# A six-layer decoder on one core: layer d's DRAM round trip and GpSimd's block inversion cut into more segments, with new work orders

## What is computed

```python
A = jnp.where(strict_lo, kb @ jnp.swapaxes(k, -1, -2), 0.0)
Tinv = solve_triangular(eye + A, eye, lower=True, unit_diagonal=True)
u = Tinv @ v
w = Tinv @ kb
# then a scan over the chunks: u_i - w_i @ S, q_i @ S + attn @ u_i, S + k_i^T @ u_i
```

## Time and profile before

| | |
|---|---|
| time, median of 3 runs | 3648.71 us (3646.90 to 3649.24) |
| the profiled execution, its own time | 3649.02 us |
| its span, first to last instruction | 3647.3 us |
| PE busy | 3133.5 us, 86% of the span |
| DVE busy | 2402.2 us, 66% |
| ACT busy | 1395.9 us, 38% |
| POOL busy | 358.3 us, 10% |
| mean granted TensorE clock | 0.893 |

### The profile page before, as it was taken

How to read it: one execution, slowest core, us unless ns; L and a number is a source line. 1 busy time by engine, 2 the same in 40 slices (tenths; PEclk the granted TensorE clock), 3 DMA queues, 4 the chain that set the end, 5 groups by cost and what they waited for, 6 DMA issues and landing times.

```text
span 3647.3 us, 49503 instructions
## 1 busy us (share of the span) xinstructions
PE 3133.5 (86%) x18500; PEld 2337.8 (64%) x18500; DVE 2402.2 (66%) x5671; ACT 1395.9 (38%) x2889; POOL 358.3 (10%) x710
## 2 busy tenths in 40 slices
PE   4788989898888989889898988989898898998765
PEld 2466767576576757667576675757667675776552
DVE  5436667585766758576675857667576775857674
ACT  2334433434444343443434343333434334342321
POOL 1002001010100101010010101001010010102110
PEclk7799899999999989999899999999999998998876
DMA  3434333234323323432342343224234322341201
GB/s 102 87 84 105 78 88 68 76 71 88 85 59 90 82 69 81 85 84 54 78 103 68 82 84 82 56 76 100 74 71 89 88 57 76 81 95 48 48 12 24
DMA packets 592813, 275.94 MB, mean 76 GB/s; under 512 B 464808, under 2 KB 555072, under 8 KB 592576
## 3 DMA queue, kind: packets, MB, share of 16 engines
q1 hardware_dynamic: 490176, 138.53, 20.1%
q10 hardware_dynamic: 102400, 134.23, 12.0%
HBM read 156.55 MB, written 14.68 MB: 47 GB/s over the span
## 4 chain that ended last, share of the span: by engine, by line
PE 54%; DVE 22%; ACT 8%; issue 6%; DMA 4%; POOL 3%; SPq 2%; ACTq 0%; DVEq 0%; POOLq 0%
PE bank L885 20%; PE bank L1089 7%; PE bank L960 6%; PE bank L937 5%; ACT pt_f L1349 3%; DVE region L1966 3%; DMA qT_f<-rest_f 2%; PE bank L920 2%; ACT split_f L1360 2%; DVE nm_f L1706 2%; PE bank L1171 2%; PE bank L1250 2%; SPq L696 2%; PE bank L952 1%; DVE yc L1890 1%
## 5 line engine op out<-in xcount | busy, mean ns | idle before, releaser
L1349 ACT ACTIVATE pt_f<-bank 128x512 f32<-128x512 f32 x768 | 418.0, 596 | 356.2 <-PE bank L937 352.3
L885 PE MATMUL bank<-xTc,c_w 128*128 128x256 f32 x2048 | 522.6, 407 | 7.8 <-DVE yc L1890 6.7
L1089 PE MATMUL bank<-c_w,c_hb 128*128 128x256 f32 x2048 | 512.0, 397 | 1.6 <-ACT c_hb L1478 0.4
L885 PEld LDWEIGHTS bank<-xTc,c_w 128*128 128x128 f32 x2048 | 404.6, 204 | 76.7 <-DVE yc L1890 10.9
L1706 DVE TENSOR_REDUCE nm_f<-bank 128x2 f32<-128x512 f32 x512 | 315.3, 683 | 206.9 <-PE bank L920 206.1
L1089 PEld LDWEIGHTS bank<-c_w,c_hb 128*128 128x128 f32 x2048 | 395.2, 200 | 64.1 <-ACT c_hb L1478 8.9
L1966 DVE SCALAR_TENSOR_TENSOR region<-vpad,cols,region 128x256 f32<-128x256 f32 x1024 | 425.4, 486 | 0.0
L937 PE MATMUL bank<-qT_f,kT_f 102*128 102x256 bf16 (+1 forms) x1536 | 305.4, 317 | 110.4 <-ACT pt_f L1349 42.2
L1478 ACT ACTIVATE c_hb<-bank,cols 128x256 f32<-128x256 f32 x512 | 214.6, 471 | 339.3 <-PE bank L885 338.8
L937 PEld LDWEIGHTS bank<-qT_f,kT_f 102*128 102x128 bf16 (+1 forms) x1536 | 121.9, 104 | 309.7 <-ACT pt_f L1349 138.9
L960 PE MATMUL bank<-pt_f,v_f 128*32 128x256 f32 x3072 | 235.8, 436 | 0.0
(11 more groups left out here) (309 smaller groups left out, 5060.2 us busy)
## 6 DMA issues: line engine op xcount, KB each, us to landing
c_w<-in_c_w ACTq DMA_DIRECT2D x256, 512.0 KB, 5.0
gram_scratch<-region SPq DMA_DIRECT2D x32, 256.0 KB, 2.3
x<-in_x SPq DMA_DIRECT2D x16, 256.0 KB, 5.7
x<-in_ctx SPq DMA_DIRECT2D x16, 256.0 KB, 5.9
ctxb<-in_ctx SPq DMA_DIRECT2D x16, 256.0 KB, 2.7
out_dram<-x SPq DMA_DIRECT2D x16, 256.0 KB, 2.2
qT_f<-split_f SPq DMA_TRANSPOSE x192, 3.4
kT_f<-split_f SPq DMA_TRANSPOSE x192, 3.4
```

What stands on the lines that cost most here:

```text
L885: mm = pe.matmul(out_ap, l, r, start=(i == 0), stop=(i == len(pairs) - 1))
L1089: mm = pe.matmul(PS[use][:, t * D:(t + 1) * D], c_hb[:, k, t * P:(t + 1) * P], c_w2[:, e % W_SLOTS, k, :], start=(k == 0), stop=(k == HC - 1))
L1349: act.activation(dst, PS[use].rearrange("p (c s) -> p c s", c=c), func, **kw).then_inc(*PS.drained(use))
```

## The change

Six new segment names. On SP `d_blocks` is divided into `d_blocks` (store A) and `d_fetch` (read the blocks back), `d_place` into `d_place` (store the inverse) and `d_begin` (read it into place). On POOL the inversion is divided into `d_blocks` (identity) and `d_solve0` to `d_solve3` (four columns each, the last with three). No instruction is added or taken away. All lists in `ORDER` but those of DVE in step 0, and of SP and POOL in steps 0 and 1, are new.

```diff
-TWO = ([... "d_gram", "d_blocks", "d_grams"]
-       + ["d_fir0", "d_place", "d_fir1", "d_fir2", "d_fir3"]
+TWO = ([... "d_gram", "d_blocks", "d_grams", "d_fetch", "d_solve0", "d_solve1"]
+       + ["d_fir0", "d_solve2", "d_solve3", "d_place", "d_begin", "d_fir1", "d_fir2", "d_fir3"]
...
     ("sync", None, """
-e_in e_turnq e_turnk e_again a_norm a_turnq d_blocks a_turnk d_place f_apply b_turnq b_turnk b_again
+e_in e_turnq e_turnk e_again a_norm a_turnq d_blocks d_fetch a_turnk d_place d_begin f_apply b_turnq b_turnk b_again
...
     ("sync", 16, """    (and the same in 17)
-e_in e_turnq e_turnk e_again d_blocks d_place f_apply
+e_in e_turnq e_turnk d_blocks e_again d_fetch d_place d_begin f_apply
...
     ("gpsimd", None, """
-a_norm e_res d_norm d_blocks f_res a_res d_out d_res c_res b_res
+d_norm a_norm d_blocks e_res d_solve0 d_solve1 d_solve2 d_solve3 f_res a_res d_out d_res c_res b_res
...
     ("tensor", None, """     (the places that differ)
-... e_score2a e_score2b e_weigh1 e_score3a c_down1b e_score3b e_weigh2 e_weigh3 d_token e_out c_up2a
+... e_score2a c_down1b e_score2b e_weigh1 e_score3a d_token e_score3b e_weigh2 e_weigh3 e_out c_up2a
-c_up2b a_norm c_down2a a_proj c_down2b f_in
+c_up2b a_norm c_down2a c_down2b a_proj f_in
-b_proj c_down5a c_down5b d_twb5 c_up6a d_one6 d_two6 d_scan0 c_up6b
+b_proj c_down5a d_twb5 d_one6 c_down5b d_two6 c_up6a d_scan0 c_up6b
...
     ("scalar", None, """
-e_score1b e_score2a e_score2b d_silu e_weigh1 e_score3a e_score3b e_weigh3 d_token
+e_score1b d_silu e_score2a e_score2b e_weigh1 e_score3a e_score3b d_token e_weigh3
-a_part1 f_up1 a_part2 c_up3a
+a_part1 f_up1 c_up3a a_part2
...
     ("vector", None, """
-e_max0 d_proj e_max1 e_max2 e_max3 e_shift c_down0b d_conv
+e_max0 e_max1 e_max2 e_max3 e_shift d_proj c_down0b d_conv
-a_rope d_norm d_gram c_down2b f_up0
+a_rope c_down2b d_norm d_gram f_up0
-f_res d_fir2 f_apply d_fir3 d_one4 d_fir4 c_down4b a_out b_ctx d_two4 a_res
+f_res d_fir2 d_fir3 f_apply d_one4 d_fir4 a_out d_two4 b_ctx c_down4b a_res
-d_two5 b_part1 b_part2 d_twb5 c_down5b d_fir6 d_sums b_max0 b_max1
+d_two5 b_part1 d_twb5 b_part2 d_fir6 c_down5b b_max0 d_sums b_max1
...
     ("vector", 16, """
-e_out e_res e_apply c_down4b f_in d_one4 d_fir4
+e_out c_down4b e_res d_one4 e_apply f_in d_fir4
     ("tensor", 16, """
-e_out c_down4a c_down4b c_up5a c_up5b d_one4
+e_out c_up5a d_one4 c_up5b d_two4
...
+                yield "d_fetch"
                 sp.wait_ge(*d_gram_out(b))
...
+                yield "d_begin"
                 sp.wait_ge(*d_zero(b))
...
-                pool.wait_ge(*d_blocks_in(b))
                 for j in range(BB - 1):
+                    if j % 4 == 0:
+                        yield f"d_solve{j // 4}"
+                    if j == 0:
+                        pool.wait_ge(*d_blocks_in(b))
```

More of the change, by code:

```diff
@@ L158 @@
     ("tensor", 1, """
[L159 to L163, removed]
+c_in a_norm c_gate a_proj c_comb c_up0a c_up0b c_down0a c_down0b c_up1a c_up1b c_down1a c_down1b c_up2a a_score0a
+c_up2b a_score0b a_score1a a_score1b a_weigh0 a_score2a a_score2b a_weigh1 a_score3a c_down2a a_score3b a_weigh2
+a_weigh3 c_down2b a_out b_in b_ctx a_res c_up3a c_up3b b_x b_proj c_down3a c_down3b c_up4a c_up4b c_down4a c_down4b
+c_up5a c_up5b b_max0 c_down5a c_down5b b_max1 c_up6a b_max2 c_up6b b_max3 c_down6a c_down6b b_again c_up7a c_up7b
+b_score0a b_score0b b_score1a b_score1b b_weigh0 b_score2a c_down7a b_score2b b_weigh1 b_score3a c_down7b b_score3b
 b_weigh2 b_weigh3 b_out b_res
@@ L166 @@
     ("tensor", 2, """
[L167 to L172, removed]
+d_in d_proj a_norm c_in c_gate a_proj c_comb c_up0a c_up0b c_down0a c_down0b c_up1a c_up1b d_token c_down1a c_down1b
+c_up2a c_up2b d_chan c_down2a c_down2b d_gram a_score0a c_up3a a_score0b c_up3b a_score1a d_grams a_score1b a_weigh0
+c_down3a a_score2a c_down3b a_score2b a_weigh1 a_score3a c_up4a a_score3b a_weigh2 a_weigh3 c_up4b a_out b_in b_ctx
+a_res d_one4 c_down4a c_down4b b_x d_two4 b_proj d_twb4 d_one5 c_up5a c_up5b d_two5 c_down5a c_down5b d_twb5 d_one6
+d_two6 c_up6a d_scan0 c_up6b d_scan1 b_max0 d_scan2 b_max1 d_scan3 b_max2 d_turn c_down6a b_max3 d_gate c_down6b
+b_again d_gated c_up7a b_score0a d_logit c_up7b b_score0b d_mix b_score1a c_down7a b_score1b b_weigh0 c_down7b
 b_score2a d_out b_score2b b_weigh1 b_score3a d_res b_score3b b_weigh2 b_weigh3 b_out b_res
@@ L226 @@
     ("vector", None, """
[L227 to L230, removed]
+e_part1 e_part2 c_gate c_comb e_max0 e_max1 e_max2 e_max3 e_shift d_proj c_down0b d_conv d_silu c_down1b d_token e_out
+a_norm e_res a_proj e_apply f_in a_rope c_down2b d_norm d_gram f_up0 a_part1 f_up1 a_part2 f_round0 c_down3b f_round1
+d_grams d_fir0 d_fir1 f_res d_fir2 d_fir3 f_apply d_one4 d_fir4 a_out d_two4 b_ctx c_down4b a_res d_twb4 a_apply
+d_one5 d_fir5 b_proj d_two5 b_part1 d_twb5 b_part2 d_fir6 c_down5b b_max0 d_sums b_max1 b_max2 d_turn b_max3 b_shift
 c_down6b d_logit d_weight d_mix d_ms d_out d_res d_apply b_out c_down7b c_res c_apply b_res b_apply
@@ L237 @@
     ("vector", 1, """
[L238 to L239 removed]
+a_norm a_proj c_gate a_rope c_comb a_part1 a_part2 c_down0b c_down1b c_down2b a_out b_ctx a_res a_apply b_proj b_part1
+c_down3b b_part2 c_down4b b_max0 c_down5b b_max1 b_max2 b_max3 b_shift c_down6b c_down7b c_res c_apply b_out b_res
 b_apply
@@ L242 @@
     ("vector", 2, """
[L243 to L246 removed]
+a_norm a_proj c_gate d_proj a_rope c_comb d_conv c_down0b d_silu a_part1 d_token a_part2 c_down1b d_norm c_down2b
+d_gram d_grams d_fir0 d_fir1 d_fir2 c_down3b d_fir3 a_out b_ctx a_res d_one4 a_apply d_fir4 d_two4 c_down4b b_proj
+d_twb4 d_one5 d_fir5 d_two5 b_part1 b_part2 c_down5b d_twb5 d_fir6 d_sums b_max0 b_max1 b_max2 b_max3 d_turn b_shift
+c_down6b d_logit d_weight d_mix d_ms d_out c_down7b d_res c_res b_out d_apply c_apply b_res b_apply
 """),
```

78 lines of the change are left out of this document (36 added, 42 removed).

## The result

The change makes the kernel faster: 3583.91 us (median of 4, 3574.12 to 3589.75) against 3647.81 us (median of 4, 3643.39 to 3649.24) beside it. The ratio is 0.9824, with a 95% interval of 0.9800 to 0.9848. The profiled execution took 3585.07 us.

The account below looks back on a forecast made before the run. PE was taken as the bound, busy 193.07 of 215.30 us a steady step, with four half-clock stretches. 3649.02 - 9 (orders) - 22 (clock) - 2 (other steps) = 3616 us; forecast 3598 to 3634, wider range 3582 to 3657.

Parts of the forecast that it names:

- the clock's term: Half-clock stretch behind `d_one6`, `d_two6` vanishes or comes later: 0 to -3.4, taken as -1.7 us a step, -22 us.
- rival 1: The slow stretch behind `d_one6`, `d_two6` goes in every steady step: 44 us in place of 22, 3594 us; chance 0.14.
- What step 2 was read to say: With an expert product behind `d_two6`, the clock falls later, in `d_scan3`; so the stretch may come 8 us later.
- The waits: New steady orders: `b_ctx` -0.75, `d_twb5` to `d_scan0` -0.25, POOL +0.3; -0.7 us a step, -9 us.
- POOL's exchange: `d_norm` ahead of `a_norm` on POOL delays a's norm: a loss of 0 to 2.9, taken as 0.3 us a step.
- The divided segments: Splitting SP's and POOL's segments costs and gains 0; f's norm still starts right behind the inversion.
- The other steps: The six steps outside the 13 steady ones: -2 us, from -8 to +6.
- PE's two waits of 9.03 us: Step 16: PE waits 6.67 us for `c_down4b` and 2.36 for the inverse; the total stays about as much.
- Rival 4: New slow stretch on PE from `e_score3b` to `e_out`: 3.4 us a step, 3682 us, in half of them 3660; chance 0.22.
- the many small idles: Many small PE idles, rather than long waits, were blamed for the slow stretch behind `d_one6`, `d_two6`; no separate size.

Follow-up runs that it names:

- scan part: The new PE and DVE order from `d_twb5` to `d_scan0` in the steady steps; alone on the kernel before, ratio 1.0002.
- e1: Kernel before with only the new PE and DVE order from `d_twb5` to `d_scan0` in the steady steps; ratio 1.0002.
- scan, heads and a_out: Reorderings of `d_twb5` to `d_scan0`; of `c_down1b`, `d_token`, `d_silu`; of `a_out`, `d_two4` ahead of `c_down4b`: alone on the kernel before, 1.0002, 0.9990, 1.0064.
- e7: Changed kernel with POOL's old steady order put back (`a_norm` ahead of `d_norm`); ratio 0.9855 to the kernel before.
- e12: Kernel before with all three steady-step reorderings (scan, heads and a_out) together; 3594.41 us, ratio 0.9849.
- e2: Kernel before with only `c_down1b` and `d_token` earlier on PE, `d_silu` and `d_token` earlier on ACT, in steady steps; ratio 0.9990.
- e8: Kernel before with only `a_out` and `d_two4` ahead of `c_down4b` on DVE in the steady steps; ratio 1.0064.
- e9: Kernel before with wasted dense fp32 products on PE per steady step, two ahead of `d_one6` and two ahead of `d_scan0`; ratio 1.0090.
- e11: Kernel before with the scan part, and `a_out` and `d_two4` ahead of `c_down4b` on DVE; ratio 0.9875.
- e16: Changed kernel with four wasted dense fp32 products per steady step ahead of layer e's first scores; 3573.32 us, ratio 0.9794 to the kernel before.

## Why the prediction was partly wrong

**The step that failed** is the size of the clock's term, "taken as -1.7 us a step", as if the stretch went in half of the steps. PE's busy time says -47.6 us, 3.7 a step, instead of 22. By the stretches' lengths, the one behind `d_two6` went in all 13 steps (44 us, rival 1's price) and came back in `d_scan2`, `d_scan3` in two (+10). And a term was missing, taken as nothing: the stretches in a's and e's heads got 30.6 and 17.5 us shorter, 24 us of work. (From `c_in` to `c_up0` 2 were lost; the sum is the 56 from above.) The time, 3583.91 us, is below the forecast's own 3598 to 3634, and in the wider range from 3582 only by 2 us, which had been drawn for rival 1. Rival 1 (3594) is nearest; it has the place and the direction, and the missing term is what it lacks.

**What step 2 was read to say** was right of the scan part by itself: in e1 the stretch does come later, in 7 of 13 steps. It doesn't hold for the whole change. The middle between the two ends stood for no mechanism; the prediction's error was to take the parts one by one. It asked of the scan part alone what it does to the clock and gave the other edits their waits only. By themselves scan, heads and a_out come to 1.0056 (product of the three ratios); together they are 0.9849.

**The waits** were right: `b_ctx` -0.78 against -0.75; `d_one6` 0.54 and twb5's 0.35 ahead of it, against "some 0.8" and "about 0.35" late; `d_scan0` 0; `d_token` still 0.95 and `e_out` 0.73. PE's idle time fell by 14.9 us, where 9 were forecast for the orders; the rest isn't traced. POOL's exchange was priced too high: in the step shown `d_norm` starts at 1773.12, so a's norm begins at 1776.03 and waits about 0.1 us for POOL, where 0.3 was taken, and e7 shows no gain from the old order.

**The divided segments**, which give the change its name, neither cost nor bring anything that shows: f's norm still starts right behind the inversion, and DVE has its wait of 7.65 us for `d_one4` as before. e12 has nearly the whole gain without them.

**The other steps**: -1.9 us against -2, by luck: it is a loss of 4.8 and a gain of 6.7. In step 16 PE's two waits of 9.03 us were said to stay about as much. PE's timeline of after has 0.77 us for the inverse and 1.04 for f's input, so that claim was wrong:

```profile
3261.51 2.05 PE L1176 MATMUL bank<-region 128*128 128x128 f32 x16 [0.77 <-DMA region<-inverse_scratch]
...
3271.99 0.66 PE L899 MATMUL bank<-ident,yf 128*128 128x128 f32 x4 [1.04 <-DVE yf L1664]
```

What steps 0 to 2 lost, 4.8 us, I haven't traced.

**Rival 4**, a new stretch from `e_score3b` to `e_out`, didn't come: e's heads have less half-clock time than before, in the 13 steps of e2 too (105.4 against 122.9). A mechanism that makes the kernel slower through the clock does exist, in another place (e8).

**The Trainium skill's rule.** The Trainium skill ("TensorE: Matmul & The Clock Gate", Part 1) puts the return of the throttle down to idleness, in its section on HAM oscillation to long waits. Behind `d_two6` the runs disagree (e9: no gap, and the stretch comes), and they disagree with the many small idles that the prediction blamed there. In e's heads they agree in part: filling 1.6 of 2.6 us of the wait took 70% of the time at half clock.

**What stays open**: why 0.78 us less wait in `b_ctx` brings a second stretch in the scan in e8 and takes it away in e11. An edit changes both what stands next to what and when each piece of work falls. No run moved the same order in time without changing or adding work, so which of the two decides where a stretch comes isn't shown. Over these 20 executions the time of the 13 steps follows the time at half clock (from 282 and 2720 to 572 and 2847 us), but no run predicts the latter from the order.

## What to carry to other kernels

Where PE is the bound and its clock falls in short stretches, price an edit of the order by the waits it removes and, apart from that, by the half-clock time over all steps: here the second was three quarters of the gain (47.6 of 62.5 us), and it did not add over parts (0, 0 and +0.6% alone, -1.5% together). So judge a set of reorderings by the set, time it, and do not throw out an edit because it is neutral or slower by itself. When a stretch is removed, look a few us further on, and at the same place in the other stages, for where it went.

## What was not expected of the hardware

- The clock fell to 0.51 behind 64x64 products that ran 3.6 us without any gap. 1.0 us of dense 256-column products ahead of them and 1.5 us behind, in which it fell, did not stop it (e9).
- Removing 0.78 us of idle time per step made the kernel 0.6% slower, by 108.8 us more at half clock (e8).
- Two us of wasted products a step, in an idle wait, cost no time that shows and cut the half-clock time of the following heads from 102.0 to 30.6 us over 13 steps (e16), but 24 us came back 70 us later in the step, in a's heads.
